# Low parts of the exps in a fused attention and mixture-of-experts kernel: which of two engines subtracts

## What is computed

```
x = x + attention(layernorm(x), context, context)      # softmax(q k / sqrt(32)) v
x = x + moe(layernorm(x))                              # top 2 of 8 experts, softmax of the two logits
# moe: y1 = rows @ w1[e].T ; gate, up = split(y1, 2) ; rows' = (silu(gate) * up) @ w2[e].T
```

## Time and profile before

| | |
|---|---|
| median of 3 runs | 9381.87 us (9380.13 to 9382.82) |
| the profiled execution | 9387.04 us, its span 9385.3 us |
| TensorE busy over the span | 8541.4 us, 91% |
| VectorE busy | 6143.3 us, 65% |
| ScalarE busy | 4576.0 us, 49% |
| GpSimd busy | 3732.8 us, 40% |
| TensorE's mean granted clock | 0.943 of full speed |

### The profile page before, as it was taken

How to read it: one execution, slowest core, us unless ns; L and a number is a source line. 1 busy time by engine, 2 the same in 40 slices (tenths; PEclk the granted TensorE clock), 3 DMA queues, 4 the chain that set the end, 5 groups by cost and what they waited for, 6 DMA issues and landing times. The chain is left out here.

```text
span 9385.3 us, 218436 instructions
## 1 busy us (share of the span) xinstructions
PE 8541.4 (91%) x75588; PEld 5030.2 (54%) x75588; DVE 6143.3 (65%) x12065; ACT 4576.0 (49%) x7066; POOL 3732.8 (40%) x4974
## 2 busy tenths in 40 slices
PE   4466669999999999999999999999999999899999
PEld 3333345555555555555555555555555555477777
DVE  7888887677777766776777767777766775222222
ACT  3466665555555555555555555555555554111111
POOL 0055554444444444444444444444444444111111
PEclk7656669999999999999999999999999999999999
DMA  9942135444445454444554444445554454466665
GB/s 366 344 176 103 51 99 149 137 141 139 140 145 147 143 146 137 144 138 137 147 147 142 143 135 144 141 138 147 147 143 142 137 144 138 130 247 242 242 246 188
DMA packets 477436, 1504.27 MB, mean 160 GB/s; under 512 B 94856, under 2 KB 115336, under 8 KB 476304
## 3 DMA queue, kind: packets, MB, share of 16 engines
q1 hardware_dynamic: 383280, 1203.45, 38.1%
q0 software_dynamic: 93152, 287.65, 12.7%
HBM read 1103.63 MB, written 407.16 MB: 161 GB/s over the span
## 5 line engine op out<-in xcount | busy, mean ns | idle before, releaser
L872 PE MATMUL e_y<-e_xt,e_w 128*128 128x512 f16 x14520 | 3518.7, 380 | 0.9 <-DMA e_w<-w_parts 0.9
L958 ACT ACTIVATE a_p<-a_sc,a_escale 128x512 f32<-128x512 f32 x2048 | 1408.2, 688 | 2289.1 <-PE a_sc L705 2213.9
L1185 POOL TENSOR_TENSOR a_pl<-a_p,a_ph 128x512 f16<-128x512 f32 x1024 | 1284.1, 1254 | 2755.3 <-ACT a_ph L959 2755.2
L1351 DVE TENSOR_REDUCE a_nmax<-a_mx 128x2 f32<-128x512 f32 x2048 | 1405.7, 687 | 1112.0 <-PE a_mx L722 1100.3
L872 PEld LDWEIGHTS e_y<-e_xt,e_w 128*128 128x128 f16 x14520 | 1372.6, 97 | 1369.7 <-issue 13.2
L893 PE MATMUL e_y<-e_w,e_yt 128*128 128x512 f16 x7480 | 1863.1, 379 | 41.4 <-DVE e_yt L1514 41.4
L959 ACT ACTIVATE a_ph<-a_sc,a_escale 128x512 f16<-128x512 f32 x2048 | 1397.2, 682 | 0.0
L705 PE MATMUL a_sc<-a_qs,a_ks 128*128 128x512 f16 x2048 | 839.9, 410 | 286.3 <-ACT a_ph L959 257.8
L893 PEld LDWEIGHTS e_y<-e_w,e_yt 128*128 128x128 f16 x7480 | 695.0, 97 | 698.0 <-issue 65.3
L722 PE MATMUL a_mx<-a_ks,a_qs 96*128 96x256 f16 x4096 | 854.9, 293 | 110.5 <-DVE a_nmax L1351 109.0
L1365 DVE COPY a_qs<-a_tr 64x1024 f16<-64x1024 f16 (+1 forms) x1024 | 702.8, 686 | 180.6 <-issue 83.7
(11 more groups left out here) (207 smaller groups left out, 11132.8 us busy)
## 6 DMA issues: line engine op xcount, KB each, us to landing
e_w<-w_parts SPq DMA_DIRECT2D x935, 512.0 KB, 3.4
h_w<-w_parts SPq DMA_DIRECT2D x425, 512.0 KB, 6.5
w_parts<-w_parts SPq DMA_DIRECT2D x136, 512.0 KB, 4.8
a_x<-in_x SPq DMA_DIRECT2D x64, 1024.0 KB, 5.0
a_xres<-in_x SPq DMA_DIRECT2D x64, 1024.0 KB, 7.5
out<-a_xres SPq DMA_DIRECT2D x64, 1024.0 KB, 7.9
xn_parts<-a_xhl SPq DMA_DIRECT2D x64, 1024.0 KB
xn_parts<-e_xg SPq DMA_DIRECT2D x56, 1024.0 KB, 13.5
```

Source lines behind the costliest of these rows:

```text
L872: last = pe.matmul(Y[:, bank, :], w1r[:, t % RING, h, pw, :], xT[:, px, h, :], start=r == 0, stop=r == 3 * HT - 1)
L958: act.activation(PF[:, q, :], SC[:, :], ACT.Exp, scale=escale[:, sp_:sp_ + 1])
L1185: pool.tensor_tensor(PL[:, kv % 2, q // 2, q % 2, :], PF[:, q, :], PH[:, kv % 2, q // 2, q % 2, :], ALU.subtract).then_inc(n["p_low"], 1)
L1351: dve.reduce_max(nmax[:, half, kv * G + 2 * gp:kv * G + 2 * gp + 2], MX[:, q % 2, :, :], AX.X, negate=True).then_inc(n["maxed"], 1)
```

## The change

GpSimd's `low_p(i, k, 1)` is taken out of its list, and VectorE gets it, right behind `max_out(i, k, 1)` and ahead of `experts(i, 8k+3)`, in every eighth. GpSimd is left with q = 0, VectorE has q = 1, 2 and 3. The counts that TensorE and ScalarE wait for are adapted: p_low now rises by 8 a batch in place of 16, p_low2 by 24. VectorE's `low_p` itself is unchanged.

```diff
@@ TensorE, values
-                pe.wait_ge(n["p_low"], b * 16 + (2 * kv + 2))
-                pe.wait_ge(p_low2, b * 16 + (2 * kv + 2))
+                pe.wait_ge(n["p_low"], b * 8 + (kv + 1))
+                pe.wait_ge(p_low2, b * 24 + (3 * kv + 3))
@@ ScalarE, exps
-                at_least(act, n["p_low"] if q < 2 else p_low2, b * 16 + (2 * kv + q % 2 - 1))
+                if q < 1:
+                    at_least(act, n["p_low"], b * 8 + kv)
+                else:
+                    at_least(act, p_low2, b * 24 + (3 * kv + q - 3))
@@ GpSimd, iteration
                     if k == 6 and on(i):
                         low_q(i, par, 1)
-                    low_p(i, k, 1)
@@ VectorE, iteration
                     max_out(i, k, 1)
+                    low_p(i, k, 1)
                     experts(i, 8 * k + 3, par, fused)
```

## The result

The changed kernel takes 9448.44 us (median of four runs; 9446.46 to 9451.29) against 9381.08 us for the kernel before (four runs): ratio 1.007, 95% interval [1.0057, 1.0083]. It is 67 us slower; the forecast was 63 us slower, 9445. The profiled executions differ by 63 us (spans of 9448.4 and 9385.3 us), and what follows is an account of these.

The account below looks back on a forecast made before the run. TensorE, busy 97% of the fused loop, was taken as the bound. The terms 51 - 12 + 8 + 16 = +63 us gave 9445 us against the median of 9381.87, 0.7% slower, with a range of 9394 to 9490 us.

Parts of the forecast that it names:

- What bounds the kernel: Fused loop: TensorE busy 97%, idle 3.6 us a step; the change acts on those 3.6 us.
- Part 1: Eighth 5 of the fused steps: the experts' low part comes 1.0 us later a step, +51 us.
- Rival C: Eighth 5, fused steps: experts' low part goes ahead of attended, costing 31 us there; sum +43, 9425 us; chance 0.15.
- Part 2: Eighth 0 of even fused steps: 1.15 us relief, less 0.68 for the new low part, -12 us.
- Part 3: Eighth 0 of odd fused steps: low part held up, exps later, a wait for maxima goes; net +8 us.
- Part 4: Other eighths of the fused steps: VectorE's extra 0.68 us is covered by its idle time, taken as 0.
- Part 5: Steps before the experts: VectorE's low part costs 1.5 us a step, mostly eighths 4 and 0, +16 us.
- B: Steps before the experts: VectorE is the bound, costing 60 us there; sum +107, 9489 us; chance 0.13.
- D: Shorter hold counts: eighth 0's relief stays whole (-46), eighth 5 costs +31; sum +1, 9383 us; chance 0.12.
- E: Faster: low part through before low_q, eighth 5 and steps before the experts cost nothing; -46, 9336 us; chance 0.08.

## Why the prediction was right, and where its parts were off

- **What bounds the kernel**: right. In the fused loop all that moved moved at the two eighths where TensorE was seen to wait for VectorE.
- **Part 1**: right in cause, and near in size in part by luck. Forecast +51, 52 in the trace; the wait for the experts' low part was to be 80 to 85 us and is 80.6. But the turn that was forecast at 1.0 us measured 0.86, 44 us in 51 steps; low_q's later end and three falls of the clock, which the sum had not, make the other 8. And the turns are no general rule, as the prediction has them. These two operations of GpSimd stand around the L1511 of the earlier trace rows:

```profile
3137.48 1.75 POOL L1185 TENSOR_TENSOR a_pl<-a_p,a_ph 128x512 f16<-128x512 f32 x1
3138.59 1.90 POOL L1158 TENSOR_TENSOR a_xres<-a_att,a_xres 128x128 f32<-128x128 f32 x2
```

L1511 had waited since 3137.80, low_p(1) ended at 3139.23, and L1511 ended only at 3140.20, 0.97 us later and not the 0.55 of a turn: the first addition, issued 0.64 us before low_p(1) ended, got in ahead of it. Behind low_q, GpSimd's next operation is issued 0.05 us before the end, and there VectorE goes first. Rival C (the experts' low part goes ahead of attended, 0.6 us) happened only where attended had been taken away, and there it gave 0.60.
- **Part 2**: right in sign, the term mis-sized. The relief was put at the length of one low part, 1.15 us. From L1426 to the second max_out it is 7.18 us before and 5.47 after (medians of 23 even steps), 1.7 less, and 2.4 less in the steps shown: with low_p(1) gone GpSimd's additions move too, and L1329 no longer waits through both (2.85 us, then 0.47). The end of L1495, behind the new low part, comes 1.1 us sooner and not 0.47. The net by the scores' starts is -1.54 a step, which makes -34 us and not -12; the 0.4 between the two is in part the clock's, and the rest is not accounted for.
- **Part 3**: right in sign, too small. That the low part would be held up was in the sum; that L1497 behind it would then be held up as well (0.6 us), by what GpSimd now does sooner, was not. +18 us and not +8.
- **Part 4**: right. The other eighths of the fused steps move by less than 0.1 us in 46 steps.
- **Part 5**: +25 against +16, within its ends, but in the wrong place: eighths 4 and 0 were named, and they make +1.0 and -1.1 of the 24.8 us; eighth 6 makes 18.9 and eighth 5 3.9.
- **The rivals**: B (VectorE the full bound before the experts, +60) fell at 25. D's relief did come whole, and more, in the even steps, but its cheap eighth 5 did not. E's condition, the low part through before low_q, was met in none of the 51 steps: it ends 0.55 us behind low_q in each.

So the sum hit by more than its parts deserve: parts 2, 3 and 5 were off by -22, +10 and +9 us, and these nearly cancel. The sign is no luck: part 1 has its cause shown by experiment. The Trainium skill (page "SBUF — State Buffer", section "Who interferes with whom") calls the port pair that the two engines share an exclusive lock, for which a VectorE instruction with two SBUF inputs contends with a GpSimd instruction that reads SBUF. The trace agrees: L1374 lasts 1.82 us behind low_q, and 0.68 alone. Read as "a shorter hold is better" (rival D) it would have given no difference, since which operation stands next in line decided more than how long each holds.

## What to carry to other kernels

Before work is moved to the faster engine, look at what stands behind its new place: 0.7 us ahead of the one operation that the bottleneck waits for cost two thirds of this loss, and the same operation one place later cost nothing. Where two engines shut each other out, follow the order in which they will wait, on both lists, and also what the engine that got lighter will now start sooner. A change over all eighths is a sum of places with both signs: the whole made the kernel 0.7% slower, and the one place that gains, taken alone, made it 0.3% faster. With the low part behind the product in eighth 0, another order on GpSimd in eighth 5 and the loop moved by 20 memsets it became 0.9%.

## What was not expected of the hardware

VectorE's idle time at the start of a pass of the fused loop depends on where the loop stands in its list. Counted in VectorE's instructions (waits for semaphores and a few others left out, so the differences are what counts), the loop's last one stands at 2364 in the kernel before, and at 2367, 2389, 2400, 2448, 2451 or 2455 in seven others: medians of 4.5 to 4.9 us. Where it stands at 2368, 2369 or 2370, in six kernels, they are 5.9 to 6.1. The place of the loop's first instruction parts the same two groups, so which of the two matters is open. Four memsets that run once made the kernel before 0.12% slower, and 19 more made the best one 21 us faster. The runs show that the place does it; why these places are slow, none of them shows.
